# LayerNorm scale by logarithm and exponential on ScalarE, and output-projection matmuls issued two steps earlier in attention

## What is computed

```python
def _layernorm(x, axis=-1, eps=1e-5):
    m = jnp.mean(x, axis=axis, keepdims=True)
    v = jnp.var(x, axis=axis, keepdims=True)
    return (x - m) / jnp.sqrt(v + eps)
...
    x = L0_attn_x                      # (8, 2048, 1024)
    xn = _layernorm(x, axis=-1)
    s = _L0_attn_ref(xn, L0_attn_Wq, L0_attn_Wk, L0_attn_Wv, L0_attn_Wo)
    g = _silu(_L0_ffn_ref(xn, ...))
    x = x + s * g
    xn = _layernorm(x, axis=-1)
    s = _L1_attn_ref(xn, L1_attn_W_qkv, L1_attn_b_qkv, L1_attn_W_out, L1_attn_b_out)
    g = _silu(_L1_ffn_ref(xn, L1_ffn_w_gate, L1_ffn_w_up, L1_ffn_w_down))
    x = x + s * g
```

## Time and profile before

| | us |
|---|---|
| three runs | 4769.5, 4782.77, 4847.44 (median 4782.77) |
| the profiled execution | 4770.72 |
| its span, from the first to the last instruction of the slowest core (core 3) | 4769.2 |
| spans of the other cores | 4740.3 to 4760.2 |

### The profile page before, as it was taken

One profiled execution on the slowest core, in us unless ns is written; L12 is line 12 of the kernel. 1 busy time (PEld: TensorE's weight loads), 2 busy tenths in 40 slices (PEclk: granted clock), 3 DMA queues, 4 the chain that ended last, 5 costly groups with the idle time before them and its releaser, 6 DMA issues.

```text
span 4769.2 us, 44345 instructions; the slowest of 8 cores (4740.3 to 4769.2 us)
## 1 busy us (share of the span) xinstructions
PE 3600.1 (75%) x14712; PEld 1437.4 (30%) x14712; DVE 1286.0 (27%) x2076; ACT 1328.3 (28%) x1573; POOL 281.6 (6%) x522
## 2 busy tenths in 40 slices
PE   2246766799999999995777777752999976677776
PEld 0012222344444444442222222211344432122221
DVE  3343320033023103303222222225211112544333
ACT  1110000011011001102666666621111100456663
POOL 1000000000000000000000000001111100000000
PEclk8578888899999999997999999965999999799997
DMA  3347677834434434431011211134444421122212
GB/s 70 65 134 202 197 211 185 209 133 144 148 133 141 150 134 140 150 141 27 12 20 36 43 37 36 34 88 117 67 75 74 76 45 27 23 55 54 45 36 66
DMA packets 139086, 450.92 MB, mean 95 GB/s; under 512 B 15568, under 2 KB 15728, under 8 KB 122480
## 3 DMA queue, kind: packets, MB, share of 16 engines
q0 software_dynamic: 73632, 218.42, 22.2%
q1 hardware_dynamic: 65232, 229.67, 13.9%
HBM read 490.23 MB, written 73.40 MB: 118 GB/s over the span
## 4 chain that ended last, share of the span: by engine, by line
PE 53%; DMA 16%; DVE 14%; ACT 10%; issue 5%; DVEq 1%; SPq 0%; POOL 0%; ACTq 0%; POOLq 0%
ACT a16t L1527 9%; PE pst L747 8%; PE pst L761 8%; PE pst L863 5%; PE pb L863 4%; DMA a32t<-l_u 4%; PE pb L1004 3%; PE pb L1467 3%; DMA a16t<-s_g 3%; PE pst L1493 2%; PE pst L940 2%; PE pst L1498 2%; PE pst L951 2%; PE pb L1472 2%; PE pst L1381 2%
## 5 line engine op out<-in xcount | busy, mean ns | idle before, releaser
L1527 ACT ACTIVATE a16t<-pst 128x1024 bf16<-128x1024 f32 x832 | 851.6, 1024 | 454.6 <-PE pst L1498 381.4
L747 PE MATMUL pst<-xn_sb,a16t 128*128 128x512 bf16 x2304 | 592.8, 404 | 187.9 <-DVE a16t L695 160.4
L761 PE MATMUL pst<-xn_sb,a16t 128*128 128x512 bf16 x2304 | 558.5, 386 | 0.0
L774 ACT ACTIVATE a32t<-pst 128x512 f32<-128x512 f32 x288 | 171.9, 597 | 1102.9 <-PE pst L747 1102.9
L782 DVE TENSOR_TENSOR a32t<-a32t,pst 128x512 f32<-128x512 f32 x256 | 175.9, 687 | 1120.4 <-PE pst L761 1114.9
L1467 PE MATMUL pb<-a16t 128*65 128x512 bf16 x832 | 333.2, 400 | 177.4 <-DVE a16t L1544 88.6
L1493 PE MATMUL pst<-a16t 128*128 128x512 bf16 x832 | 339.3, 408 | 163.2 <-DVE a16t L1426 103.5
L747 PEld LDWEIGHTS pst<-xn_sb,a16t 128*128 128x128 bf16 x2304 | 226.1, 102 | 504.9 <-issue 285.5
L1498 PE MATMUL pst<-a16t 128*128 128x512 bf16 x832 | 340.1, 409 | 0.0
L1472 PE MATMUL pb<-a16t 128*65 128x512 bf16 x832 | 331.0, 398 | 0.0
L761 PEld LDWEIGHTS pst<-xn_sb,a16t 128*128 128x128 bf16 x2304 | 230.4, 100 | 289.7 <-issue 32.0
(11 more groups left out here) (156 smaller groups left out, 2785.2 us busy)
## 6 DMA issues: line engine op xcount, KB each, us to landing
a16t<-s_g POOLq DMA_DIRECT2D x108, 512.0 KB, 5.1
a16t<-s_u SPq DMA_DIRECT2D x108, 512.0 KB, 4.0
a32t<-l_u SPq DMA_DIRECT2D x32, 1024.0 KB, 9.4
a16t<-s_d SPq DMA_DIRECT2D x27, 1024.0 KB, 5.2
a16t<-s_d POOLq DMA_DIRECT2D x27, 1024.0 KB, 5.2
s_g<-a16t SPq DMA_DIRECT2D x36, 512.0 KB, 7.2
s_u<-a16t SPq DMA_DIRECT2D x36, 512.0 KB, 7.8
s_d<-a16t SPq DMA_DIRECT2D x18, 1024.0 KB, 7.6
```

Of the source, the lines that this page charges most:

```text
L747: li = t.matmul(pb[gp_][:, :], a16t[:, o_gb[wp] + hc * 256 + ici * 128: o_gb[wp] + hc * 256 + ici * 128 + 128], xn_sb[:, hc * T + tc * TC: ...
L761: li = t.matmul(pb[up_][:, :], a16t[:, o_ub[wp] + hc * 256 + ici * 128: o_ub[wp] + hc * 256 + ici * 128 + 128], xn_sb[:, hc * T + tc * TC: ...
L1527: return s.activation(a16t[:, o_pt[kp4]:o_pt[kp4] + 2 * TC], pst[kp][:, 0:1024], AF.Exp, scale=0.125)
```

## The change

Two edits that have nothing to do with each other.

In phase A the square root on ScalarE and the reciprocal on VectorE are replaced by a logarithm and an exponential on ScalarE: 1/sqrt(v + eps) = exp(-0.5 * ln(v + eps)). In phase C units may be added from block 4 on instead of block 6, one in each step, and two in a step only in the last two blocks instead of the last three.

```diff
-                op_sqrt = P.add("S", lambda s: s.activation(
-                    a32t[0:1, o_t1:o_t1 + TC], a32t[0:1, o_var:o_var + TC],
-                    AF.Sqrt, bias=cst32[0:1, C_EPS:C_EPS + 1]),
-                    deps=[op_srow], name=f"A{L}sqrt{tc}")
+                def f_sqrt(s):
+                    s.activation(a32t[0:1, o_t1:o_t1 + TC],
+                                 a32t[0:1, o_var:o_var + TC],
+                                 AF.Ln, bias=cst32[0:1, C_EPS:C_EPS + 1])
+                    s.drain()
+                    return s.activation(a32t[0:1, o_rstd:o_rstd + TC],
+                                        a32t[0:1, o_t1:o_t1 + TC],
+                                        AF.Exp, scale=-0.5)
+                op_sqrt = P.add("S", f_sqrt, deps=[op_srow],
+                                name=f"A{L}rsq{tc}")
 
                 def f_rstd(v):
-                    v.reciprocal(a32t[0:1, o_rstd:o_rstd + TC],
-                                 a32t[0:1, o_t1:o_t1 + TC])
-                    v.drain()
                     return v.scalar_tensor_tensor(
@@
-                        if kc >= 6:
+                        if kc >= 4:
                             emit_unit()
-                            if kc >= nkc - 3:
+                            if kc >= nkc - 2:
                                 emit_unit()
```

## The result

| | before | changed |
|---|---|---|
| median of all runs, us | 4783.8 (13 runs) | 4752.3 (12 runs) |
| lowest run, us | 4765.6 | 4734.7 |

The ratio of the changed kernel to the one before is 0.9947, with a 95% interval from 0.9927 to 0.9968. Of 4784 us that is 25 us less, between 15 and 35. The forecast was 24.7 us less. By the bound of 2% it counts as no change, but the interval leaves out 1.

A forecast was written before the change was run, and what follows sets the result against it. No engine was taken to bound the whole, each stage having its own limit; phase A is a serial chain. Gains of 21.8 + 1.3 + 1.6 = 24.7 us from 4770.7 gave 4746.0 us, with an 8-in-10 range of 4726 to 4774.

The forecast's parts named there:

- Part 1 and 2: Phase A: logarithm/exponential pair 1.52 us instead of 4.24, 21.8 us gained over eight chunks; one A1 table load saved, 1.3 us.
- Part 3: Phase C: moved units change only their place; net 1.6 us gained, between 5.0 gained and 5.0 lost.
- Second: Layer 1, second chunk, passes of 8 blocks: two fewer units in the tail, 0.36 us a pass, 2.9 us gained.
- Third: Layer 1, third chunk, passes of 12 blocks: two more unmasked steps carry a unit, 0.16 us a pass, 1.3 us lost.
- Fourth, and layer 0: Passes of layer 1's fourth chunk and layer 0's chunks 1 to 3: net 0, the fourth within 1.6 us either way.
- the clock rivals: Layer-0 passes: earlier units spare TensorE's low clock (19 us gained, chance 0.08) or bring more of it (34 us lost, 0.07).
- Tables split: Phase A: exponential and logarithm in different tables, 11 more loads, 14.3 us, and no load saved; 4761.6 us, chance 0.06.
- Phase A hidden: Phase A: loads of x take up the gain in half the chunks, 11 of 21.8 us lost; 4757 us, chance 0.09.

The follow-up runs named there:

- the repeated ratio: The changed kernel measured again with no edit, against the kernel before: ratio 0.9978 [0.9946, 1.0010].
- the units alone: The kernel before with only the units moved, square root and reciprocal kept: one comparable execution, 4787.5 us, no ratio.
- the scale row alone: The changed kernel with the units back where they were, only the logarithm/exponential edit left: ratio to before 0.9945 [0.9920, 0.9971].
- the shorter chain: The changed kernel with phase A's variance in one instruction and scale and shift rows written straight in bf16, two casts dropped: ratio to before 0.9905 [0.9877, 0.9932].
- the third buffer: The kernel with phase A's variance fused and casts dropped, plus a third buffer for the second load of x: ratio 0.9807 [0.9761, 0.9852], median 4697.0 us.

## Why the prediction was right

The forecast was right in its mechanism and in its sum. Two slips in it did not count, and the closeness of the total (25 against 24.7 us) is in part luck: its interval goes from 15 to 35, and the repeated ratio gives 11 us, between 5 lost and 26 gained. The stages are the better witness, with 12.0 + 10.9 + 4.0 = 26.9 us.

**Part 1 and 2, phase A.** The price of the pair was right to 0.01 us (1.53 against 1.52), and the load of A1 went. One step of the working does not follow as written: at 1.02 us for 1024 columns, 512 would be 0.51 and not 0.43 us. But in the changed kernel the exponential takes 1.06 us on a row of 1024 and 0.63 on one of 512, so 0.43 is what the rows have. By the steps 10.9 us should go from A0 and 10.9 + 1.3 = 12.2 from A1. One profile isn't exact enough to test that, but seven can be used. Two kernels have the square root (before, and the units alone): on the average A0 284.8, A1 148.8. Five have the new pair and nothing else in phase A: 272.8 and 137.9. So 12.0 us went from A0 and 10.9 from A1, 22.9 in all where the steps have 23.1. That A1, with the saved load, gained less than A0 lies within the scatter of A1 (136.5 to 139.4 in those five, 147.1 and 150.4 in those two). The first weight cast of layer 0, forecast 11 us earlier than 292.24, starts at 280.27, 12 us earlier, though on another core.

**Part 3, the units.** The forecast was a net 1.6 us gained. C1 is 648.2 us on the average of the two kernels with the old units (before, and the scale row alone) and 644.2 on that of the five with the new ones, the one with the low clock in its fourth chunk left out: 4.0 us gained, within the bounds of 5.0 either way, and 2.5 gained with that one counted. Chunk by chunk:
- Second: 0.36 us a pass was forecast, 2.9 in all. Measured are 145.6 - 143.0 = 2.6, or 145.4 - 142.5 = 2.9 as the averages of the two kernels with the old units and the six with the new ones; and 0.28 a pass at full clock, the lower end of the net given. The tail became 0.43 shorter, and the two moved units take back 0.15.
- Third: 1.3 us lost was forecast. The step is priced right: the shortest pass went from 21.74 to 21.90, 0.16 us longer. The sum does not show it. It is 180.8 and 179.8 with the old units, and 178.8, 180.8, 178.8, 179.5, 181.4 and 181.5 with the new ones, in the order of the tables. How many passes ran at full clock throughout decides more than the units: 72 of 128 in this chunk with the old units, 163 of 256 with the new ones, but 24 of 32 in the changed kernel and 17 of 32 in the shorter chain, which has the same units. In the second chunk it is 79 of 128 against 187 of 256. So neither the loss of 1.3 us nor a gain by the clock is shown in this chunk, and why the units' place should matter for the clock stays open.
- Fourth, and layer 0: no change was forecast, and 217.2 became 216.8; of the five other kernels with the new units four have 216.3 to 218.5, and one 222.3 at the low clock. In layer 0 the sums of the three chunks are 226.0, 226.6 and 225.7 before and 225.3, 225.9 and 225.6 after. TensorE does not wait at the unit of block 4.

**The rivals.** Of the 24 passes a core that carry units in layer 0, a share of 0.28 had a clock of 0.88 before, 0.26 with the scale row alone, 0.25 in both profiles of the change, and 0.29 with the units alone. That is 6 or 7 of 24. The forecast's 48 passes with units are those of both layers; a core has 24 in layer 0, 9 of them at 0.88 by the share that it read. With 24 the clock rivals come to 9 x 1.1 = 10 us gained and 15 x 1.1 = 17 us lost, so the second could not have made the change slower. Neither came, as the share did not move. Tables split: there are 12 loads and none in the pair, and the kernel that forces two there gives the price. Phase A hidden: 22.9 of 23.1 us arrived, so the loads did not take up the gain. B0, which would have had to give it back, moved by 6 us between two profiles of the changed kernel, and they lie on either side of the kernel before's.

What the forecast read, that the chain is DMA for long pieces of phase A, was true and led only to a rival of 0.09: between 3165 and 3320 us, in phase A1, loads of x_res for the normalisation are 37% of core 5's chain in the changed kernel. These loads move along with the one-row chain, so they hide nothing of it. But they were also the larger reserve, as the third buffer showed.

## What to carry to other kernels

Where engines take turns in a serial chain on short rows, each instruction counts nearly in full, and a change there can be priced from the rows to a tenth of a us; count the table loads of both versions first, since two of them would have cost what the reciprocal's removal saved. Before shortening the arithmetic of such a chain, look at what ends the idle time of the large instructions beside it: one more buffer for the loads was worth 37 us, more than the change and the shorter chain together (23 and 11). A piece of work that rides on another engine's slack should be spread one in a step from the first step where its input is ready and the other engine has a lead; earlier than that it cost here what it saved at the end.

## What was not expected

- The third buffer had been expected to bring some 10 us in A0 and 10 to 20 in A1, and brought 15.5 and 21.3. With two buffers the load of a tile is issued only when the tile two places before it is used up. That this leaves a load too little time is the reading of the waits; a fourth buffer was not tried, and 20.1 us of waiting for loads are left.
- Moving units out of the tail has an end: in blocks 2 and 3 they cost 0.26 us each on the average, more than the 0.215 us that a unit takes itself, because the first waits for its input.
- Stage B0 (TensorE is busy for 441 of its first 628 us in core 5 of the changed kernel, while weights are loaded, and for 1181 of the 1248 us behind them) came out anywhere between 1868.1 and 1882.0 us in kernels with the same code for it. That is more than half of the change's gain, so the median of few runs and the span of one core could not have told the two edits apart; the stages could.
